# GpSimd's products by B in a Mamba scan: seven products by a per-partition scalar become tensor-tensor products with B's column broadcast

## What is computed

```
def step(h, inp):
    u_t, d_t, b_t, c_t = inp
    dA = jnp.exp(d_t[:, :, None] * A)
    h = dA * h + (d_t * u_t)[:, :, None] * b_t[:, None, :]
    y = jnp.einsum('bdn,bn->bd', h, c_t)
```

## Time and profile before

| | |
|---|---|
| three runs | 2141.48, 2144.67, 2146.16 us |
| median | 2144.67 us |
| profiled execution: span | 2143.5 us |
| scans of the four layers, first to last | 54.4 to 1708.8 us |
| VectorE, TensorE, ScalarE, GpSimd busy | 91%, 88%, 79%, 68% of the span |
| GpSimd's products by a scalar (L472) | 896 instructions |
| GpSimd's products with B broadcast (L469) | 128 instructions |

### The profile page before, as it was taken

How to read it: one execution, slowest core, us unless ns; L and a number is a source line. 1 busy time by engine, 2 the same in 40 slices (tenths; PEclk the granted TensorE clock), 3 DMA queues, 4 the chain that set the end, 5 groups by cost and what they waited for, 6 DMA issues and landing times.

```text
span 2143.5 us, 34659 instructions
## 1 busy us (share of the span) xinstructions
PE 1877.8 (88%) x10816; PEld 1183.1 (55%) x10816; DVE 1943.2 (91%) x1826; ACT 1683.8 (79%) x3053; POOL 1458.1 (68%) x1364
## 2 busy tenths in 40 slices
PE   4788888888888888888888888888888799999998
PEld 1444444444444444444444445444444499989998
DVE  3799999999999999999999999999999987767775
ACT  4899999899999998989999999999999433333333
POOL 2688888888888888888888988888889600000000
PEclk9899999999999999999999999999999999999999
DMA  7323232323232323232333333332322200000000
GB/s 241 86 64 79 63 78 62 78 62 78 62 79 63 80 65 79 64 79 65 81 78 73 81 76 79 78 78 62 78 62 72 84 1 11 11 12 11 11 6 11
DMA packets 72786, 138.55 MB, mean 65 GB/s; under 512 B 13072, under 2 KB 31120, under 8 KB 68112
## 3 DMA queue, kind: packets, MB, share of 16 engines
q1 hardware_dynamic: 66320, 119.28, 22.7%
q10 hardware_dynamic: 6400, 18.42, 3.7%
HBM read 63.85 MB, written 7.74 MB: 33 GB/s over the span
## 4 chain that ended last, share of the span: by engine, by line
ACT 27%; PE 26%; POOL 26%; issue 13%; DVE 6%; ACTq 1%; SPq 1%; DMA 1%; POOLq 0%; DVEq 0%
POOL scan L478 12%; POOL scan L472 11%; PE y_ps L1291 11%; ACT decay L563 10%; PE dbu_ps L1266 8%; ACT scan L641 6%; DVE scan L829 3%; POOL scan L469 2%; PE dbu_ps L1067 2%; ACT sp_e L600 2%; ACT delta L601 2%; ACT sp_l L610 2%; PE y_ps L1052 2%; ACT sp_e L605 1%; ACT du_t L626 1%
## 5 line engine op out<-in xcount | busy, mean ns | idle before, releaser
L829 DVE TENSOR_TENSOR_SCAN scan<-decay,dbu_ps 128x1024 f32<-128x1024 f32 x512 | 1154.6, 2274 | 29.8 <-PE dbu_ps L1067 21.9
L1067 PE MATMUL dbu_ps<-ident,scan 128*128 128x128 f32 x4096 | 571.6, 286 | 220.7 <-DVE scan L829 195.9
L478 POOL TENSOR_TENSOR scan<-scan,c_rep 128x1024 f32<-128x1024 f32 x255 | 671.8, 2635 | 130.4 <-ACT du_t L626 66.5
L1067 PEld LDWEIGHTS dbu_ps<-ident,scan 128*128 128x128 f32 x4096 | 482.2, 147 | 500.1 <-DVE scan L829 259.3
L563 ACT ACTIVATE decay<-d_rep,a_cur 128x510 f32<-128x510 f32 x1024 | 668.0, 709 | 54.1 <-POOL scan L478 15.7
L472 POOL TENSOR_SCALAR scan<-du_t,b_t 128x256 f32<-128x256 f32 x896 | 594.8, 679 | 0.0
L641 ACT ACTIVATE scan<-du_t,b_t 128x256 f32<-128x256 f32 x1024 | 445.6, 494 | 1.2
L838 DVE TENSOR_TENSOR scan<-scan,c_rep 128x1024 f32<-128x1024 f32 x257 | 331.0, 1288 | 0.0
L766 ACT ACTIVATE decay<-dbu_ps 128x512 f32<-128x512 f32 x256 | 147.9, 597 | 205.2 <-PE dbu_ps L1266 183.1
L1052 PE MATMUL y_ps<-scan,sel 128*32 128x512 f32 x2048 | 299.8, 661 | 0.0
L1080 PE MATMUL pre_ps<-xn,w_pre 128*128 128x512 f32 x512 | 245.5, 603 | 5.2 <-DVE w_pre L818 5.2
(11 more groups left out here) (110 smaller groups left out, 1648.8 us busy)
## 6 DMA issues: line engine op xcount, KB each, us to landing
d_rep<-delta SPq DMA_DIRECT2D x496, 128.0 KB, 2.9
c_rep<-c_rows SPq DMA_DIRECT2D x32, 1024.0 KB
w_pre<-prepared_weights ACTq DMA_DIRECT2D x15, 866.0 KB, 13.0
prepared_weights<-scan SPq DMA_DIRECT2D x3, 1122.0 KB, 12.9
scan<-in_conv_w SPq DMA_DIRECT2D x4, 512.0 KB, 5.0
w_out<-prepared_weights SPq DMA_DIRECT2D x16, 128.0 KB, 12.5
sp_e<-in_x_rows SPq DMA_DIRECT2D x8, 256.0 KB, 3.2
d_rep<-in_w ACTq DMA_DIRECT2D x2, 1024.0 KB, 6.8
```

The costliest lines, as they stand in the source:

```text
L478: nc.gpsimd.tensor_tensor(ring[slot % RING], ring[slot % RING], c_rep[par][:, slot // PRS, :].unsqueeze(1).broadcast_to([128, 2, TG]), ALU ...
L829: nc.vector.tensor_tensor_scan(ring[slot % RING].rearrange("p u t -> p (u t)"), decay[slot % DEC].rearrange("p u a t -> p (u a t)"), dbu_p ...
L1067: last = nc.tensor.transpose(dbu_ps[slot % 2][:, u, 128 * j:128 * j + 128], dbu_t[m % 2][:, j, b, :, :].rearrange("p q c -> p (q c)"), ide ...
```

## The change

In `outer` of GpSimd, the branch on `q == 0 and j == 0` goes. All eight products of a group of states are now made as the first one was: a tensor-tensor multiplication of `du_t` (128 partitions x 256 elements) by B's column, which is read with a step of zero over the 256 elements. Before, seven of the eight were `tensor_scalar` instructions, with the column as a scalar per partition and a second multiplication by 1.0. Order, buffers, waits and semaphores stay as they are, and ScalarE's eight products too.

```
-                    if q == 0 and j == 0:
-                        nc.gpsimd.tensor_tensor(dst, src, col.unsqueeze(2).broadcast_to([128, UNITS, CH]), ALU.mult)\
-                            .then_inc(dbut_pool, 1)
-                    else:
-                        nc.gpsimd.tensor_scalar(dst, src, col, 1.0, ALU.mult, ALU.mult).then_inc(dbut_pool, 1)
+                    nc.gpsimd.tensor_tensor(dst, src, col.unsqueeze(2).broadcast_to([128, UNITS, CH]), ALU.mult)\
+                        .then_inc(dbut_pool, 1)
```

## The result

The changed kernel takes 2179.09 us (median of four runs) against 2144.47 for the kernel before in the same comparison: 1.0156 times as long, 95% interval 1.0140 to 1.0172. That is 34.6 us slower, where 37 were forecast.

What follows compares the result with a forecast made beforehand. A loop through ScalarE, GpSimd, TensorE and VectorE was taken as the bound. Per window, 1.0 us (group 0's leg) plus 0.2 (VectorE's hold), 31 times, added 37 us to the 2143.5 span: median 2181, range 2147 to 2212.

Steps and rivals of the forecast that it cites:

- The loop and its leg: Four-engine loop per window: du_t copies to group 0's eighth product has no slack and grows about 1.0 us.
- One step of the walk: Slot 13: VectorE's product finds GpSimd's fourth product under way and ends 0.46 us later.
- The sum: Per window 1.0 us from group 0 plus 0.2 from VectorE's product of slot 3; 31 windows, 37 us.
- The start of the leg: GpSimd waits for exactly ScalarE's copies of du_t, having been idle 2.47 us when it started at 616.76.
- The price of a product: Each changed GpSimd product takes 0.14 us longer; the 28 of a window make 3.9 us more work.
- VectorE's hold: Slot 3: VectorE's product meets GpSimd's longer products under way, costing between nothing and 0.6 us; 0.2 taken.
- The same in slot 5 and later: From slot 5 on, VectorE being held by GpSimd's products falls in its wait for ScalarE and costs nothing.
- Rival (a): VectorE does not hold GpSimd's 256-element tensor-tensor form, making the time shorter: 2137 us, chance 0.08.
- Rival (b): GpSimd's idle time and VectorE's lock hide the longer products: 2145 us, chance 0.10.
- Rival (c): Slot 1: late GpSimd product by C delays VectorE's product up to 2.3 us: 2.0 a window, 2207 us, chance 0.17.

Runs made afterwards that it cites:

- the two cuts of group 0: Kernel before, tensor-tensor form in group 0 for slot 13's four products only, or the four of slots 14 and 15: 2151.45 and 2158.30 us.
- the short leg with the tensor-tensor form: Changed kernel with GpSimd's product by C of slot 13 moved behind group 0's eighth product: 2177.31 us.
- the second move on both forms: Slot 7's product by C also put ahead of slot 8's products, beside slot 13's moved behind group 0's eighth: 2170.98 us on changed kernel, 2150.15 on before.
- the short-leg kernel with groups 1 to 3 changed: Kernel before with slot 13's product by C moved behind group 0's eighth product, and tensor-tensor form in groups 1 to 3 only: 2165.33 us.

## Why the prediction was right, and where it wasn't

**The loop and its leg.** Right in the changed kernel. The leg from the copies of `du_t` to the eighth product grew by 0.99 us, where 1.02 and 0.97 had been walked. The two legs behind it, up to the scan of slot 2, did not change, and the window grew by 1.2 us as summed. The scans took 1689 us from first to last, forecast 1692. VectorE idles ahead of the scan of slot 2 in 30 of 31 windows, 0.42 us in the median, as said. One step of the walk did not come about: VectorE's product of slot 13 was to end 0.46 us later. Its mean is 1319 ns before and 1317 after, over 28 windows. The leg's growth is what seven products at 0.14 us make by themselves, 0.98 us.

**The sum.** In part luck. The forecast was 31 us from group 0 and 6 from VectorE's hold. Alone, group 0 cost 23.7, and the other groups 13.2. The first term was 7 us too large and the second 7 too small, and the two misses cancel in the total of 34.6 against 37.

**The start of the leg.** Wrong as told. It was said that GpSimd waits for exactly the copies of `du_t`. With the wait moved nothing changed: the scan of slot 11 and VectorE's product next to it hold GpSimd's product by C until the same moment. VectorE feeds the leg as well as ScalarE does, and the forecast did not hang on which.

**The price of a product.** Right within the noise: 0.14 us each was taken; the leg of the changed kernel gives 0.14, and the two cuts of group 0 gave 0.10 and 0.13 a window.

**VectorE's hold.** The term was partly in the wrong places, and too small where groups 1 to 3 stand alone. In slot 3, 0.2 us were taken; the product by C there has a mean of 1336 ns over 27 windows where it had 1199, 0.14 us. "The same in slot 5 and later falls in VectorE's wait for ScalarE, and costs nothing" fails twice. In slot 5 the product by C went from 1199 to 1266 ns. And it fails for what comes behind that wait: the second and the third softplus instruction went from 1380 to 1519 and from 1235 to 1499 ns, 0.14 and 0.26 us a window or 12.5 us in all. They were not in the sum. In the loop as walked they lie beside ScalarE's leg, whose 25.66 us did not grow; in VectorE's account they are three quarters of the hold. That both accounts come to the same time is likely because the routes are nearly equal, since the scan of slot 2 waits only 0.42 us for TensorE; it wasn't tested. With the leg shortened, the hold makes the whole difference of the two forms in VectorE's account (56.9 us more, and 5.4 less wait).

**Rival (a), that VectorE doesn't hold this form.** Refuted. Of the 1024 products, 245 take over 1 us (185 before). One that started inside VectorE's product of 1110.42:

```profile
1110.59 1.60 POOL L468 TENSOR_TENSOR scan<-du_t,b_t 128x256 f32<-128x256 f32 x1
...
1110.42 1.29 DVE L835 TENSOR_TENSOR scan<-scan,c_rep 128x1024 f32<-128x1024 f32 x1
```

It takes 1.60 us instead of 0.61. The Trainium skill's rule in SBUF — State Buffer, "Who interferes with whom", that a VectorE instruction with two SBUF inputs and a GpSimd instruction that reads SBUF exclude each other, agrees with this row.

**Rival (b), that the longer products are hidden.** Refuted by the time, 34.6 us longer, and by TensorE's 1.39 us of idle time ahead of the first transposes, where before it was 0.81 and 0.56.

**Rival (c), a long product by C in VectorE's way.** It did not come about in slot 1, nor anywhere in the changed kernel: no product by C of VectorE takes over 1669 ns there. But the mechanism is real and near. It shows in three of the experiments (the short leg with the tensor-tensor form, and the second move on both forms), at the first softplus instruction (2.91 us), and at the product of slot 8 (2.90). It was priced at one place, slot 1, and there it never came.

**Still open.** Group 0 alone cost 23.7 us where 31 were expected; its leg grew by 0.78 instead of 0.99 us. With only the other groups changed the same leg is 9.83 us, 0.15 longer than before, so their form lengthens it too; through which collision was not followed. That the groups' shares change with the leg (24 and 13 us, then 14 and 43) is measured and fits the account; which single collision makes which part was followed only in the windows shown. And nothing was run in which GpSimd's total work stays and its longer instructions all stand where VectorE has none with two SBUF tiles; that would separate the single collisions from the total of the two engines.

## What to carry to other kernels

Where two engines shut each other out, price a longer instruction three times: in its own leg, in what the other engine waits for when it meets it under way, and in the idle time that it eats and that so far let the other engine go first. An idle time has a last releaser, and often a second one just before it; before moving a wait, ask when the second one comes. Add up what two such engines need together, each moment once: where that is nearly the whole stretch, an order that avoids one collision makes another. And if a wait ahead of the busiest engine is removed and the time does not move, sum that engine's durations as well as its gaps: the same instructions may have grown by what the gaps have lost.

## What the runs showed of the hardware that was not expected

"Whichever starts first keeps the other out" is not all. In the kernel with groups 1 to 3 changed, one product by C of VectorE took 7.28 us instead of 1.19. The timeline of GpSimd and VectorE there:

```profile
1143.04 2.33 POOL L469 TENSOR_TENSOR scan<-du_t,b_t 128x256 f32<-128x256 f32 x4
1145.33 2.35 POOL L478 TENSOR_TENSOR scan<-scan,c_rep 128x1024 f32<-128x1024 f32 x1
1147.64 2.33 POOL L469 TENSOR_TENSOR scan<-du_t,b_t 128x256 f32<-128x256 f32 x4
...
1143.76 7.28 DVE L838 TENSOR_TENSOR scan<-scan,c_rep 128x1024 f32<-128x1024 f32 x1
```

GpSimd started seven more instructions while VectorE's was pending, two of the first row and all of the other two (none of them lengthened), and VectorE's ended at 1151.04, 1.07 us after the last of them. So a waiting VectorE does not always get the next turn between two GpSimd instructions in a row. It happened once in that kernel and twice in the short-leg kernel with groups 1 to 3 changed, and in neither kernel of the case.
